# Gated delta rule: tables straight from PSUM, resets scaled by beta, unit matrix added into the tables, residual in one step

## The reference

```
kk = kk / max(norm(kk), 1e-12)
Sk    = einsum('bhi,bhipj->bhpj', k_t, state)
delta = (v_t - Sk) * b_t
state = state * d_t + einsum('bhi,bhpj->bhipj', k_t, delta)
o     = einsum('bhi,bhipj->bhpj', q_t, state)
out   = silu(z) * rmsnorm(o);  y = out @ W_out.T
```

## Time and profile before

| | |
|---|---|
| median of 3 runs | 4521.77 us |
| profiled execution | 4521.22 us, span 4519.4 us |
| TensorE matmul busy | 3998.6 us, 88% |
| VectorE busy | 3161.6 us, 70% |
| ScalarE busy | 2237.8 us, 50% |
| GpSimd busy | 1898.3 us, 42% |
| recurrent stage | about 100 to 3080 us of the span |

### The profile page before, as it was taken

The page is one execution under the profiler, slowest core; times in us unless marked ns, Lnnn a source line. Parts: engine busy times, 40 slices in busy tenths (PEclk is TensorE's granted clock), DMA queues, the critical chain, the costliest instruction groups (busy, mean ns, idle before and its releaser), DMA issues. The chain is left out here.

```text
span 4519.4 us, 75144 instructions
## 1 busy us (share of the span) xinstructions
PE 3998.6 (88%) x26288; PEld 2920.6 (65%) x26288; DVE 3161.6 (70%) x5082; ACT 2237.8 (50%) x4061; POOL 1898.3 (42%) x1852
## 2 busy tenths in 40 slices
PE   3899999999999999999999999995788989389998
PEld 2677777777776777767777777774344444178887
DVE  3788888888888888888888888884556556632222
ACT  1465655556565655656565565653344445221111
POOL 1365554545455554545455454543233333311110
PEclk8899999999999999999999999997799999699999
DMA  2001010101001011010101010101565563000001
GB/s 74 15 29 36 25 36 21 41 25 32 29 20 41 24 32 30 29 32 24 32 30 36 25 36 21 29 27 31 94 91 90 83 92 60 38 24 19 19 14 38
DMA packets 134066, 172.39 MB, mean 38 GB/s; under 512 B 12524, under 2 KB 79980, under 8 KB 133132
## 3 DMA queue, kind: packets, MB, share of 16 engines
q1 hardware_dynamic: 131212, 166.03, 15.9%
q10 hardware_dynamic: 2432, 1.05, 0.2%
HBM read 143.12 MB, written 21.76 MB: 36 GB/s over the span
## 5 line engine op out<-in xcount | busy, mean ns | idle before, releaser
L405 PE MATMUL pj<-xh,w_hi 128*128 128x512 f32 x1536 | 686.1, 447 | 26.3 <-ACT conv_k L612 17.8
L990 POOL TENSOR_TENSOR silu_z<-silu_z,exp_z 128x512 f32<-128x512 f32 x128 | 184.6, 1442 | 1216.9 <-ACT exp_z L629 1216.9
L405 PE MATMUL pj<-xh,w_lo 128*128 128x512 f32 x1536 | 608.0, 396 | 0.0
L405 PE MATMUL pj<-xl,w_hi 128*128 128x512 f32 x1536 | 603.3, 393 | 0.0
L1518 DVE TENSOR_REDUCE row_max<-s 128x1 f32<-128x512 f32 x512 | 341.9, 686 | 271.8 <-PE s L1272 268.6
L975 POOL TENSOR_SCALAR b_t<-qk_masked,beta_section 128x256 f32<-128x256 f32 (+1 forms) x512 | 490.5, 968 | 21.5 <-ACT qk_masked L714 20.2
L1452 ACT ACTIVATE probs<-s 128x512 f32<-128x512 f32 x512 | 291.3, 595 | 325.0 <-PE s L1296 319.4
L756 DVE SCALAR_TENSOR_TENSOR conv_v<-conv_in,conv_w_section,conv_v 128x512 f32<-128x512 f32 x384 | 403.7, 1051 | 20.2 <-ACT conv_v L612 9.1
L680 ACT ACTIVATE kk_masked<-tp 128x512 f16<-128x512 f32 x320 | 191.5, 598 | 323.7 <-PE tp L496 320.2
L405 PEld LDWEIGHTS pj<-xh,w_hi 128*128 128x128 f32 x1536 | 291.8, 190 | 83.3 <-issue 31.2
L405 PEld LDWEIGHTS pj<-xh,w_lo 128*128 128x128 f32 x1536 | 289.6, 189 | 67.4
(11 more groups left out here) (259 smaller groups left out, 10250.9 us busy)
## 6 DMA issues: line engine op xcount, KB each, us to landing
w_raw<-in_w_in SPq DMA_DIRECT2D x128, 256.0 KB, 3.5
decays<-decay_by_head SPq DMA_DIRECT2D x64, 512.0 KB, 3.8
decays<-decay_by_head SPq DMA_DIRECT2D x64, 256.0 KB, 4.9
q_stack<-qk_parts SPq DMA_DIRECT2D x128, 128.0 KB
k_stack<-qk_parts SPq DMA_DIRECT2D x128, 128.0 KB
f_raw<-in_f_w SPq DMA_DIRECT2D x32, 256.0 KB, 2.7
x_all<-in_x SPq DMA_DIRECT2D x4, 1024.0 KB, 11.5
source<-in_ctx SPq DMA_DIRECT2D x8, 512.0 KB
```

The source lines that it names most:

```text
L405: mm = pe.matmul(pj[j % 2][:, :], a[:, j, k * P:(k + 1) * P], b[:, k, bp * WIN:(bp + 1) * WIN], start=(n == 0), stop=(n == 3 * KT - 1))
```

## The change

The unit matrix moves from the scan's constant into data: ScalarE writes `beta_diag`, the diagonal scaled by beta, eight 128x128 copies per section (`act_beta`), so the scan gives decays already times beta. The tables then are one product each, of decays with the PSUM bank of the matmul (`dve_table`), and both a_t and b_t are VectorE's; `act_kq` and `pool_b` are gone. VectorE adds the unit matrix into the diagonal blocks of a_t (`dve_inverse`), and ScalarE writes their negative as the inverse's matrix (`act_minus`); the level masks carry the opposite sign on the diagonal. With the unit in a_t the residual is v minus one product, and `dve_rest` goes. At levels 5 and 6 ScalarE copies only the blocks that are not zero (`act_x`) where VectorE masked. The low halves of the gated output move from GpSimd to VectorE. The k products with k run earlier on TensorE, and those with q later. `t_i` and `u_i` of chunk 0 get a tile of their own.

```diff
         tp, up = m.ps("tp"), m.ps("up")
         ms = [m.ps(f"ms{i}") for i in range(2)]
         tu_bank = (tp, ms[1])
+        kq_bank, sum_bank = (ms[0], ms[1], up, ms[0]), (tp, ms[1])
...
-                E["km"].wait(pe, t, 0)
-            bank = (ms[0], ms[1], up, ms[0])[i]
-            right, o = (kn, cv[QUERY])[i % 2], (i // 2) * SEQ
+                E["at"].wait(pe, t, 1)
+            bank, right, o = kq_bank[i], (kn, cv[QUERY])[i // 2], (i % 2) * SEQ
...
             if more:
-                E["km"].wait(pe, s + 1, 3)
-            pe.matmul(ms[p][:, :], ones, osq[p][:, :], start=True, stop=True).then_inc(E["oss"].sem, 1)
+                E["at"].wait(pe, s + 1, 3)
+            pe.matmul(sum_bank[p][:, :], ones, osq[p][:, :], start=True, stop=True).then_inc(E["oss"].sem, 1)
...
 
         def pe_tu(pe, s, lv, c):
 
-            E["xm"].wait(pe, s, 2 * (lv - 1) + c)
+            if lv < WIDE:
+                E["xm"].wait(pe, s, 2 * (lv - 1) + c)
+            else:
+                E["xa"].wait(pe, s, 2 * c + 1 if lv == WIDE else 4 + c)
...
             proj(GATE, 1)
             E["delta"].wait(pe, s, 0)
             pe_group(pe, up, lambda q: a_t[:, q, P:SEQ], delta[0], "cp")
-            proj(GATE + 1, 0)
-            E["rhs1r"].wait(pe, s, 0)
             E["uc"].wait(pe, s, 1)
-            pe_group(pe, xp[0], lambda q: u_f[:, 1, mat(q)], v_r, "d0p")
-            proj(GATE + 1, 1)
-            E["d0"].wait(pe, s, 1)
-            pe_group(pe, xp[1], lambda q: a_t[:, q, SEQ:TRI], d0[:, :].bitcast(F32), "rp")
             if nxt:
                 pe_kq(pe, s + 1, 0)
                 pe_kq(pe, s + 1, 1)
+            E["rhs1r"].wait(pe, s, 0)
+            pe_group(pe, xp[0], lambda q: u_f[:, 1, mat(q)], v_r, "d0p")
+            proj(GATE + 1, 0)
+            E["d0"].wait(pe, s, 1)
+            pe_group(pe, xp[1], lambda q: a_t[:, q, SEQ:TRI], d0[:, :].bitcast(F32), "rp")
+            proj(GATE + 1, 1)
```

```diff
+        def act_minus(act, s, c):
+            E["ia"].wait(act, s, c)
+            act.activation(by_mat(a_n[:, c, :]), a_t[:, :, (slice(0, P), slice(SEQ, TRI))[c]], ACT.Copy, scale=-1.0)\
+               .then_inc(E["an"].sem, 1)
+
         def act_section(act, s, bp, hk, prev, nxt):
+            for c in range(2):
+                act_minus(act, s, c)
...
+                if lv >= WIDE:
+                    for c in range(2):
+                        act_x(act, s, lv, c)
...
+                    if nxt:
+                        act_beta(act, s + 1)
...
             act_gate(act, s, 1)
             act_sigmoid(act, s, 0)
-            if nxt:
-                act_kq(act, s + 1, 0)
-                act_kq(act, s + 1, 1)
-                act_kq(act, s + 1, 2)
-                act_kq(act, s + 1, 3)
             act_sigmoid(act, s, 1)
 
-        def act_kq(act, t, i):
-            E["kq"].wait(act, t, i)
-            act.activation((kk, qk)[i % 2][:, i // 2, :], (ms[0], ms[1], up, ms[0])[i][:, 0:TRI], ACT.Copy)\
-                .then_inc(E["km"].sem, 1)
...
+        def act_x(act, s, lv, c):
+
+            E["xp"].wait(act, s, 2 * (lv - 1) + c)
+            b = 1 << lv
+            for n in range(P // (2 * b)):
+                rows = slice(2 * b * n + b, 2 * b * (n + 1))
+                act.activation(by_mat(x_l[c][lv - 1][rows, :])[:, :, 2 * b * n:2 * b * n + b],
+                               xp[c][rows, 0:H].rearrange("p (m n i) -> p m n i", m=NM, i=b)[:, :, n, :], ACT.Copy)\
+                   .then_inc(E["xa"].sem, 1)
+
+        def act_beta(act, t):
+
+            E["beta_s"].wait(act, t, 0)
+            E["dec"].wait_before(act, t)
+            for q in range(NM):
+                for c in range(2):
+                    o = c * (SEQ + 1) + 1
+                    act.activation(beta_diag[:, slot(q), o:o + P], ident, ACT.Copy,
+                                   scale=beta_s[:, 2 * (q // PV) + c, q % PV:q % PV + 1]).then_inc(E["bd"].sem, 1)
```

```diff
+                E["bd"].wait(dve, t, 7)
             i = slot(q)
-            dve.tensor_tensor_scan(dec[:, i, :], dec[:, i, :], diag, 0.0, ALU.mult, ALU.add).then_inc(E["dec"].sem, 1)
...
+            dve.tensor_tensor_scan(dec[:, i, :], dec[:, i, :], beta_diag[:, i, :], 0.0, ALU.mult, ALU.add).then_inc(E["dec"].sem, 1)
+
+        def dve_table(dve, t, b, c, out, kq, done, after):
+
+            E["kq"].wait(dve, t, kq)
+            E["dec"].wait(dve, t, b * PV + PV - 1)
+            sl = (slice(0, SEQ), slice(SEQ, TRI))[c]
+            o = c + after
+            dve.tensor_tensor(out[:, b * PV:(b + 1) * PV, sl], dec[:, b:NM:2, sl.start + o:sl.stop + o],
+                              kq_bank[kq][:, sl].unsqueeze(1).to_broadcast([P, PV, sl.stop - sl.start]), ALU.mult)\
+               .then_inc(E[done].sem, 1)
+
+        def dve_a(dve, t, b, c):
+            dve_table(dve, t, b, c, a_t, b, "at", 0)
+
+        def dve_b(dve, s, prev):
+            if prev:
+                E["op"].wait(dve, s + -1, PV - 1)
+            for b in range(2):
+                for c in range(2):
+                    dve_table(dve, s, b, c, b_t, 2 + b, "bt", 1)
+
+        def dve_gated_rest(dve, s, p):
+            E["ghi"].wait(dve, s, p)
+            dve.tensor_tensor(g_lo[p][:, :], gat[p][:, :], g_hi[p][:, :].bitcast(F32), ALU.subtract)\
+                .then_inc(E["glo"].sem, 1)
+
+        def dve_inverse(dve, s):
+
+            E["at"].wait(dve, s, 3)
+            for sl in (slice(0, P), slice(SEQ, TRI)):
+                dve.tensor_tensor(a_t[:, :, sl], a_t[:, :, sl], ident.unsqueeze(1).to_broadcast([P, NM, P]), ALU.add)\
+                   .then_inc(E["ia"].sem, 1)
```

```diff
                 E["vr"].wait(dve, s, 0)
-            dve.tensor_tensor(v_t[:, c, :], v_t[:, c, :], d0[:, :].bitcast(F32), ALU.subtract)\
-               .then_inc(E["rd0"].sem, 1)
-
-        def dve_residual(dve, s, c):
-
-            E["rd0"].wait(dve, s, c)
...
-            dve_beta(dve, s, bp, hk)
-            dve_a(dve, s)
+            dve_inverse(dve, s)
+            dve_b(dve, s, prev)
             if prev:
                 dve_gated(dve, s + -1)
             if nxt:
                 dve_conv_weights(dve, t, nhk)
+                dve_beta(dve, t, nbp, nhk)
             for lv in range(1, LEVELS):
...
+                for c in range(2 if lv < WIDE else 0):
...
+                if lv == 2 and prev:
+                    for p in range(PV):
+                        dve_gated_rest(dve, s + -1, p)
...
+            if nxt:
+                dve_decays(dve, t, 1)
             dve_gate(dve, s, 0)
             if nxt:
-                dve_decays(dve, t, 1)
-            dve_rest(dve, s, 1)
+                dve_a(dve, t, 0, 0)
+            dve_residual(dve, s, 1)
             if nxt:
+                dve_a(dve, t, 0, 1)
                 dve_decays(dve, t, 2)
-            dve_residual(dve, s, 1)
+            E["dp2"].wait(dve, s, 1)
+            dve.tensor_tensor(delta[1], tp[:, :], d0[:, :].bitcast(F32), ALU.add).then_inc(E["delta"].sem, 1)
             dve_gate(dve, s, 1)
             if nxt:
                 dve_decays(dve, t, 3)
-            E["dp2"].wait(dve, s, 1)
-            dve.tensor_tensor(delta[1], tp[:, :], d0[:, :].bitcast(F32), ALU.add).then_inc(E["delta"].sem, 1)
+                dve_a(dve, t, 1, 0)
+                dve_a(dve, t, 1, 1)
...
-        def pool_b(pool, s, q):
-            E["km"].wait(pool, s, q // PV * 2 + 1)
-            E["beta_s"].wait(pool, s, 0)
-            if s:
-                E["op"].wait(pool, s - 1, PV - 1)
-            for c, sl in enumerate((slice(0, SEQ), slice(SEQ, TRI))):
-                pool.tensor_scalar(b_t[:, q, sl], qk[:, q // PV, sl], beta_s[:, 2 * (q // PV) + c, q % PV:q % PV + 1],
-                                   None, ALU.mult).then_inc(E["bq"].sem, 1)
-            E["dec"].wait(pool, s, q)
-            E["bq"].wait(pool, s, 2 * q + 1)
-            pool.tensor_tensor(b_t[:, q, 0:SEQ], b_t[:, q, 0:SEQ], dec[:, slot(q), 1:SEQ + 1], ALU.mult)\
-                .then_inc(E["bt0"].sem, 1)
-            pool.tensor_tensor(b_t[:, q, SEQ:], b_t[:, q, SEQ:], dec[:, slot(q), SEQ + 2:], ALU.mult).then_inc(E["bt"].sem, 1)
-
-        def pool_gated_rest(pool, s, p):
-            E["ghi"].wait(pool, s, p)
-            pool.tensor_tensor(g_lo[p][:, :], gat[p][:, :], g_hi[p][:, :].bitcast(F32), ALU.subtract)\
-                .then_inc(E["glo"].sem, 1)
```

More of the change, by code:

```diff
@@ L292, in delta_net @@
         NM = 2 * PV
+        WIDE = 5
         WC = KT * P
@@ L308, in delta_net @@
         v_r = m.sb("rhs_rounded", [P, NM * P], F32R)
-        kk = m.sb("kk_masked", [P, 2, TRI])
-        qk = m.sb("qk_masked", [P, 2, TRI])
+        tu0 = m.sb("t_and_u0", [P, 2 * NM * P], F16)
+        beta_diag = m.sb("beta_diag", [P, NM, TRI + 2])
         dec = m.sb("decays", [P, NM, TRI + 2])
@@ L467, in pe_first @@
             E["u0"].wait(pe, s, c)
-            if c == 0 and after_out:
-                E["delta"].wait(pe, s + -1, 1)
-            elif after_out:
-                E["oln"].wait(pe, s + -1, 1)
```

(45 more changed lines are left out.)

37 lines of the change are left out of this document (18 added, 19 removed).

## The result

The changed kernel takes 4682.68 us (median of four runs, 4670.26 to 4682.9) against 4521.20 before (four runs): ratio 1.035, 95% interval 1.0332 to 1.0368. It is 161 us slower where 47 were forecast, and outside the range.

What follows compares the result with a forecast made beforehand. TensorE was taken to bound the recurrent stage, so only its waits count: 4521 + 54 (ordinary crossings) + 1 (into a head) - 3 (splits) - 4.5 (stage ends) = 4568 us, slower by 1.0%, range 4480 to 4625.

Steps and rivals of the forecast that it cites:

- The ordinary crossing: From one section's key-norm matmul to the next's, without head change: +1.15 us each, 47 of them, +54 us.
- level 3: Level 3 combine on TensorE: VectorE's low halves and query taps make its mask late, +0.55 us, bounds 0 and +1.1.
- level 5: TensorE's level 5 wait: eight beta copies on ScalarE precede the blocks, +0.4 us, bounds -0.4 and +1.2.
- The norm wait: TensorE's output-norm matmuls wait for squares behind negations and blocked adds: +2.1 us, bounds +0.95 and 0.5 more blocking.
- The rival of adds that slip past the silu products: VectorE's adds run unblocked by GpSimd, squares 1.15 us sooner per crossing, 71 us less, 4497; chance 0.14.
- ScalarE's 31 and GpSimd's 8 busy us a section: Signs expected in the new profile: ScalarE busy 31 us a section, GpSimd under 8.
- VectorE's 31: Sign expected in the new profile: VectorE busy near 31 us a section.
- the prediction's own 2 us less: VectorE's operations removed against those added: about 2 us less work per section, by like rows.
- The rule that the prediction set aside: ScalarE's fixed 224 cycles plus one per element from SBUF: beta copies 0.3 us each, sum 20 us higher.
- Sum +0.05 each, +1 us: 15 crossings into a head, with the loop's jump: squares 3.0 us later, offset by waits that end.
- 2.95 us of old waits: In crossings into a head: 0.95 at key projection and transposes, 2.0 on taps blocked by splits, would end.
- 0.5 of the 46.20 comes back, 0.3 is lost on taps of the key: Weight splits moved forward in two sections of a head: -3 us over 16 heads.

Runs made afterwards that it cites:

- the held version: Changed kernel, all work kept, GpSimd's weight splits of each head's first and third sections held until VectorE has masked level 3: 4598.37 us, ratio 1.017.
- the best version: Changed kernel with squares first, beta copies spread, low halves behind level 3, second silu product after the adds, third-section splits held: 4391.41 us, ratio 0.971.

## Why the prediction was right in sign and wrong in size

**The ordinary crossing was read well.** The starts of TensorE's matmuls, counted from the start of a crossing of median length (45.55 us before, 46.91 after), give each term:

| place | before | after | running difference | the term | forecast |
|---|---|---|---|---|---|
| output norms (L445, L448) | 16.96 | 18.82 | +1.86 | +1.86 | +0.1 and +2.1 |
| first transposes (L473, L474) | 20.55 | 22.04 | +1.49 | -0.37 | -0.4 |
| level 1 combine | 24.48 | 25.66 | +1.18 | -0.31 | -0.3 |
| level 2 combine | 28.57 | 29.34 | +0.77 | -0.41 | -0.4 |
| level 3 combine | 32.34 | 33.46 | +1.12 | +0.35 | +0.55 |
| output projection | 35.02 | 35.76 | +0.74 | -0.38 | -0.4 |
| level 5, last combine | 41.10 | 42.98 | +1.88 | +1.14 | +0.4 |
| level 6 combine | 43.97 | 45.33 | +1.36 | -0.52 | -0.5 |

The sum is +1.36 against +1.15. Seven terms are within 0.35. That the sum comes so close is in part luck: level 5 is 0.74 too low, the norms are 0.34 and level 3 is 0.20 too high. The norm wait came out of the chain that the prediction wrote down: add 2 blocked, negation behind it, square behind that. The rival of adds that slip past the silu products did not happen; the run with the small silu product shows that its price was right. Of the signs, ScalarE's 31 and GpSimd's 8 busy us a section came true (30.9 and 7.3); VectorE's 31 did not. It has 35.5 where it had 39.0, and the prediction's own 2 us less would have given 37.

**Level 5 was mis-sized.** The prediction took 0.26 us for a beta copy and 0.15 for a block. The eight copies take 2.44 us, 0.305 each, and the four blocks 1.15, 0.29 each: 0.36 and 0.56 us more, 0.9 in all. That would make the term +1.3; the table has +1.14, just under the far bound of +1.2. The nearest row was an 8x128 activation, and the fall from its record to a 0.15 step was the guess. A record of a copy lasts 0.395 and of a block 0.27. The rule that the prediction set aside, the fixed cost in the Trainium skill, "VectorE: DVE Perf Modes", section on the TRN2 errata, makes the copy 0.3 us by estimate; the timeline agrees, with 0.305 from start to start.

**"Sum +0.05 each, +1 us" for the loop's crossings is the first step that failed.** In a crossing of median length (48.06 us before, 52.04 after) the squares' norm matmuls started 3.06 us later (18.32 to 21.38), against 3.0 forecast. But then the granted clock fell: from the norm matmuls to the transposes TensorE took 5.73 us where the ordinary crossing takes 3.22, 2.5 us that the prediction had at nothing. TensorE has no idle time in between in either, so this is the clock alone. It was not in the sum at all, because every row read had 1.00. Of the 2.95 us of old waits that should have ended, 2.2 did; level 5 took 1.1 and level 6 gave 0.5: 3.06 + 2.5 - 2.2 + 1.1 - 0.5 = 4.0. The run with the squares first agrees: with that wait gone its first crossing has a clock of 1.00 and is 3.63 us shorter. The 2.6 that this is more than in the ordinary ones is not the clock's alone, since this wait was longer and new ones came.

**"0.5 of the 46.20 comes back, 0.3 is lost on taps of the key" is the second.** The prediction named the old collision that ends when the splits move, and of the new place only the taps of the key. But they start when their weights land and not when GpSimd is free, so they meet the query taps too, and the level 3 combine waits 2.98 us. A third crossing of 50.78 us (before 46.35) is 2.08 late at the norms, 0.98 at level 2, 4.04 at level 3 and 5.32 at the level 4 products, the last 1.2 with matmuls at half clock again (0.63 us records from 1233.15). Holding the splits or shrinking them brings 84 and 87 us, 53 and 52 of them in the third crossings (16 times 3.3), and 34 and 32 in the first ones, where the first split no longer meets the adds.

**How much was clock.** The mean granted clock of the stage's 3080 us is 0.98 after and 1.00 before; 2% of 3080 is some 60 us. With rounding that is 46 to 77 us, so 30 to 50% of the loss. That is an estimate from a mean. The clock record of the two traces, summed, puts it in the middle: 147 us of the stage at 0.50, and 24 before, which is 73 and 12 us lost, 61 more or 38% of the loss, at most, since TensorE also waits within them. The clean prices are the 1.59 us of the held version's fourth crossing and the 2.5 us above.

**What stays open.** Why the clock falls after a given wait and not after another like it. After the change it fell behind all 13 norm waits from 2.8 to 3.5 us and all four of 3.0 at level 3, behind four of the seven of 2.5 there, and behind 6 of 49 norm waits of 1.8 to 1.9; in the held version it fell behind 12 of 51 of these. The runs give no rule, and none was tried for itself. Nor was it taken apart why the best version's first crossing is still 2 us longer than an ordinary one; of the third's 3.3 the rows above show 2.9.
